# Moving the first denominator group of each half by four slots, and taking the last quad's first reciprocal from the bank

## The reference

```python
q = Wq @ layernorm(x) + bq;  k = Wk @ ctx + bk;  v = Wv @ ctx + bv
dot = mask * (q . k) / sqrt(32) - (1 - mask) * 1e6
amap = softmax(dot, axis=-1) * mask          # a row maximum, exp, and a denominator
x = x + tanh(g_xattn) * (amap @ v)
x = x + tanh(g_ffn) * fp8_product(layernorm(x), W2)
```

## Time and profile before

| | us |
|---|---|
| median of 3 runs | 2485.4 (2483.09 to 2494.34) |
| the profiled execution, its own time | 2483.92 |
| its span, first to last instruction | 2482.1 |
| TensorE busy | 2406.5 |
| VectorE busy | 1934.1 |
| ScalarE busy | 1401.9 |
| GpSimd busy | 1714.9 |
| mean granted TensorE clock | 0.994 of full |

### The profile page before, as it was taken

The page is one execution under the profiler, slowest core; times in us unless marked ns, Lnnn a source line. Parts: engine busy times, 40 slices in busy tenths (PEclk is TensorE's granted clock), DMA queues, the critical chain, the costliest instruction groups (busy, mean ns, idle before and its releaser), DMA issues. The chain is left out here.

```text
span 2482.1 us, 40026 instructions
## 1 busy us (share of the span) xinstructions
PE 2406.5 (97%) x12612; PEld 1362.3 (55%) x12673; DVE 1934.1 (78%) x3196; ACT 1401.9 (56%) x2702; POOL 1714.9 (69%) x1413
## 2 busy tenths in 40 slices
PE   7999999999999999999999999999999999999996
PEld 5888888875444444444444444444444444444442
DVE  6777666677788888888888888888888888888874
ACT  3333333325666666666666666666666666666663
POOL 2443333436887878888887888888788787878873
PEclk9999999999999999999999999999999999999998
DMA  6766666665566666666666666666666666666633
GB/s 238 256 241 234 232 235 233 237 204 145 121 128 141 134 133 129 139 139 137 128 130 131 138 135 128 127 131 137 137 129 129 137 139 129 133 135 138 139 75 73
DMA packets 265487, 380.57 MB, mean 153 GB/s; under 512 B 77688, under 2 KB 145336, under 8 KB 257112
## 3 DMA queue, kind: packets, MB, share of 16 engines
q1 hardware_dynamic: 245240, 275.57, 46.1%
q0 software_dynamic: 9216, 67.11, 13.5%
q10 hardware_dynamic: 10848, 35.66, 4.1%
HBM read 199.83 MB, written 101.38 MB: 121 GB/s over the span
## 5 line engine op out<-in xcount | busy, mean ns | idle before, releaser
L1251 DVE TENSOR_REDUCE part_max<-bank 128x1 f32<-128x512 f32 x2048 | 1282.8, 683 | 254.0 <-PE bank L978 247.5
L790 ACT ACTIVATE probs<-bank 128x512 f32<-128x512 f32 x2048 | 1077.6, 602 | 595.9 <-PE bank L961 579.4
L961 PE MATMUL bank<-q_st,k_st 100*128 100x512 f32 x2048 | 866.9, 425 | 4.5 <-ACT probs L790 3.3
L978 PE MATMUL bank<-k_st,q_st 98*128 98x512 f32 x2048 | 816.6, 399 | 6.0 <-DVE part_max L1251 4.7
L441 POOL TENSOR_TENSOR pair_sum<-probs 128x512 f32<-128x512 f32 x512 | 641.9, 1283 | 134.3 <-ACT probs L790 134.1
L961 PEld LDWEIGHTS bank<-q_st,k_st 100*128 100x128 f32 x2048 | 387.2, 189 | 411.7 <-issue 190.3
L993 PE MATMUL bank<-probs,v_t 128*32 128x512 f32 x4096 | 545.5, 605 | 0.0
L978 PEld LDWEIGHTS bank<-k_st,q_st 98*128 98x128 f32 x2048 | 387.9, 189 | 128.2 <-DVE part_max L1251 19.1
L441 POOL TENSOR_TENSOR stage_hi<-probs 128x512 f32<-128x512 f32 x252 | 316.1, 1287 | 75.6 <-ACT probs L790 75.4
L441 POOL TENSOR_TENSOR stage<-probs 128x512 f32<-128x512 f32 x252 | 318.2, 1325 | 24.9 <-ACT probs L790 24.9
L402 POOL TENSOR_TENSOR stage_lo<-stage,stage_hi 128x512 fp32r<-128x512 f32 x128 | 188.3, 1492 | 137.8 <-ACT stage_hi L735 136.7
(11 more groups left out here) (121 smaller groups left out, 2360.1 us busy)
## 6 DMA issues: line engine op xcount, KB each, us to landing
pair_sum<-pair_sum POOLq DMA_DIRECT2D x64, 1024.0 KB, 8.5
k_st<-k_scr SPq DMA_DIRECT2D x192, 256.0 KB
q_st<-q_scr SPq DMA_DIRECT2D x192, 256.0 KB
c_raw<-in_ctx_dram ACTq DMA_DIRECT2D x32, 512.0 KB, 7.0
k_scr<-stage_hi SPq DMA_DIRECT2D x64, 256.0 KB, 2.5
k_scr<-stage_lo SPq DMA_DIRECT2D x64, 256.0 KB, 2.7
v_scr<-stage SPq DMA_DIRECT2D x64, 256.0 KB, 2.9
q_scr<-stage_hi SPq DMA_DIRECT2D x64, 256.0 KB, 2.4
```

The source lines that it names most:

```text
L790: nc.scalar.activation(probs[:, c % PR, h, :], s_bank_of(n, k)[:, :], ACT.Exp).then_inc(exp_done, 1)
L961: nc.tensor.matmul(s_bank_of(n, k)[:, :], k_st[p][0:KS, h, j * P:(j + 1) * P], q_st[p][0:KS, th, h, :], start=True, stop=True).then_inc(sc ...
L978: nc.tensor.matmul(x_bank_of(n, "tile", k)[:, :], q_st[p][0:KX, th, h, tc * P:(tc + 1) * P], k_st[p][0:KX, h, sh * HALF:(sh + 1) * HALF], ...
L1251: nc.vector.tensor_reduce(part_max[:, th, at:at + 1, sh], x_bank_of(n, "tile", k)[:, :], AX, ALU.max).then_inc(max_done, 2)
```

## The change

The first group of each half is issued at slots 31 and 63 in place of 27 and 59. In the last quad alone, the copy, the two moves through HBM, the small reciprocal and the mask product of the first half are left out; VectorE takes the reciprocal of all 512 columns from d_bank and multiplies by mask and gate, in its queue at slot 45. The pair 6 products of the last quad (`denominators_last(SJ - 2)`, with the first group of the half, so at slot 63 too) wait for that reciprocal in place of the copy.

```diff
-            DEN_AT = {27: 0, 35: 1, 43: 2, 59: 3}
+            DEN_AT = {31: 0, 35: 1, 43: 2, 63: 3}
...
-                            if r == (5 if n == LAST else 6) and real(n):
+                            if r == 6 and ordinary(n):
                                 mask_inverse(n, 0)
...
-                        if real(n):
+                        if ordinary(n):
                             move_den(n, 0)
...
-                        if real(n):
+                        if ordinary(n):
                             move_inv(n, 0)
                             spread_inv(n, 0)
...
-                            if k == 44 and real(n):
+                            if k == 44 and ordinary(n):
                                 copy_den(n, 0)
...
                         if r == SJ - 2:
-                            pe.wait_ge(den_copied, 2 * LAST + 1)
+                            pe.wait_ge(last_inverse, 1)
...
+                    def invert_last():
+
+                        dve.wait_ge(den_done, NG * LAST + GROUPS_0)
+                        dve.wait_ge(half_weighed, LAST)
+                        nc.vector.reciprocal(inv_b[:, 0], d_bank[:, :]).then_inc(last_inverse, 1)
+                        dve.wait_ge(last_inverse, 1)
+                        nc.vector.scalar_tensor_tensor(inv_b[:, 0], inv_b[:, 0], g1[:, 0:1], m_b[:, 0:HALF], ALU.mult,
+                                                       ALU.mult).then_inc(last_inverse, 1)
...
-                        dve.wait_ge(inv_spread[0], 16 * (m + 1))
+                        dve.wait_ge(last_inverse, 2)
...
-                        if k == 51 and real(n):
+                        if k == 51 and ordinary(n):
                             invert(n, 0)
+                        if k == 45 and n == LAST:
+                            invert_last()
```

More of the change, by code:

```diff
@@ L202, in flamingo_gated_layer @@
         half_weighed = sem("half_weighed")
+        last_inverse = sem("last_inverse")
         norm_done = sem("norm_done")
@@ L325, in flamingo_gated_layer @@
             F_JOBS = {23: "max1", 39: "ffn0", 51: "ffn1", 55: "max0"}
-            DEN_AT = {27: 0, 35: 1, 43: 2, 59: 3}
+            DEN_AT = {31: 0, 35: 1, 43: 2, 63: 3}
             DEN_AFTER = {3: 4, 11: 5}
-            NG = 6
+            NG, GROUPS_0 = 6, 3
             SUM_OF_GROUP = (2, 1, 3, 6, 5, 7)
```

## The result

The change makes the kernel 0.29% slower by the recorded ratio, 1.0029 with a 95% interval of 1.0021 to 1.0036. The medians are 2492.04 us over 20 runs and 2486.48 over 20 runs of the kernel before beside them (5.6 us, or 0.22%, apart). Of the latter, one run took 3821.61 us and the others 2480.2 to 2494.3; the ratios here go by the fast runs alone. The prediction was 2485 and no change. The profiled execution has a span of 2492.4 us at a mean clock of 0.992, 10.3 above the one before.

What follows compares the result with a forecast made beforehand. TensorE, busy 97%, was taken to bound the kernel: its queue plus its waits. 2483.92 + 4 (steady part) - 3.5 (finish) = 2484.4, given as 2485 with the median's offset; range 2468 to 2497 for 8 times in 10.

Steps and rivals of the forecast that it cites:

- no change: Whole kernel: 2485 us; a measurement was said to tell 0.5%, 12 us, from no change; chance of same 0.7.
- the bank wait: Slots 63 and 31: fourth score tile waits for VectorE's late maximum; per period 0.25 us lost at 63, 0.07 gained at 31.
- rival 2: Slots 59 to 63: GpSimd's adds shut out VectorE's L93, about 5 us each; chance 0.03 all periods (2634), 0.07 some.
- rival 1: Slots 63 and 31: the bank wait doesn't bite, 2456 us, chance 0.13; a half of it, about 2470, chance 0.11.
- rival 3: Slots 31 and 63: denominators come too late for their later uses, some 0.5 us per period, 2500 us; chance 0.02.
- some odd period: Single periods: GpSimd's adds shut VectorE out, +5 us in a single one, 2490 to 2510; chance 0.07.
- the margin of 0.48: Behind slot 59: L93 starts at 1444.66, 0.48 us ahead of GpSimd's pair 7 adds at 1445.14, so it gets in first.
- One add at most: Port pair shared by VectorE and GpSimd: by the skill's lock rule, VectorE would lose one GpSimd add at most.
- The term of -3.5: Last quad's finish: residual lands 3.2, say 3.5 us earlier, without the spread inverse's wait; bounds 0.8 to 8.0.
- the 0.9 that I had taken off: Finish: 0.9 us off the residual load's 6.5, as it no longer shares queues with the spread's 256 KB.
- The steady sum: Slots 63 and 31 over all periods: about +4 us; bounds -24.5 to +10.7.
- the 1.25 for quads 0 and 1: Three groups (quad 0 both halves, quad 1 the first) without VectorE steps beside them: win 0.46 + 0.33 + 0.46 us.

Runs made afterwards that it cites:

- Experiment 5: The changed kernel with quad 1's group at slot 59 and VectorE's four steps (L90, L93, L100, L101) cut to 128 of 1024 columns above quad 0: 2461.45 us, ratio 0.9907.
- the control of experiment 5: The kernel before, groups at slots 27 and 59, with the same four VectorE steps cut to 128 of 1024 columns: 2483.58 us, ratio 0.9998.
- experiment 3: The changed kernel with, in quad 1 alone, the second half's first group back at slot 59: 2487.36 us, ratio 1.0004 to the kernel before.
- experiment 1: Each half alone against the kernel before: moved slots only, 2499.03 us, ratio 1.0048; last quad's inverse only, groups at 27 and 59, 2479.33 us, ratio 0.9970.
- experiment 6: VectorE's steps spread, last quad changed; L95 cut at 512 or 768 columns. Moved groups (quad 1's at 59): 0.9971, 0.9937; old slots: 1.0027, 0.9995, against the kernel before.

## Why the prediction was wrong

**What held.** The group starts without a wait; slots 63 and 31 have the bank wait; the stretches moved by +0.25 (forecast +0.25) and by -0.10 (forecast -0.07); L1324 (L1314 before) waits for nothing, L1327 (L1317 before) for the residual. Experiment 5 and its control show that this wait is the cause. It was not the whole-period version of rival 2, nor rival 1, nor rival 3.

**What failed first: rival 2 in "some odd period".** I gave it a chance of 0.07 and 5 us, and nothing in the sum. It comes in quad 1 in every kernel profiled whose group stands at slot 63 there (7.26, 7.53, 7.31 and 7.28 for L90) and in none with it at 59. It costs 8.0 us in the trace and about 6 by the runs (experiment 3). Both the price and the place were off. Beside the standstill of 6.9 us, products and group then ran at half clock. And two parts of my reasoning let it through. I weighed the margin of 0.48 in one period and took it for all, though GpSimd is later against TensorE in quad 1: in the kernel before, its sum for `stage` is ready 2.52 behind the start of the products of slot 59 there, and 1.06 in a usual period. And I looked at L93 against the adds of pair 7, while it was L90, begun amid those of pair 6, that counted. The wait that I took away was what gave GpSimd its pause. Why GpSimd is late just in quad 1 stays open. It has no feed-forward products yet (the first one comes at 718.8 us in the kernel before), but quad 0 has none either, and there the sum is 1.20 behind; no run adds or removes them.

The Trainium skill (SBUF — State Buffer, "SBUF: two separate sides") has the port pair that VectorE and GpSimd share as a lock: whoever starts first holds it for the instruction, and the other is blocked in full. The trace agrees with the block: L90 took 7.26 us against 0.68. "One add at most" was my own step from it, and that failed: L90 was shut out over the end of one block of adds and the whole of another, though each add is an instruction of its own, and it ended only behind GpSimd's last one.

**What failed second: the finish.** The term of -3.5 (3.2 by its parts, rounded up) measured -5.9 in the trace and about -7.5 by the runs (bounds 0.8 to 8.0). The store was 1.5 earlier, the number forecast, but by luck: I put it down to the moved group, and 1.2 of it comes with the group at its old slot too (experiment 1, and the control of experiment 5), because what it makes up is the fall of the clock in the one execution I read. I took that fall, the 1.93 in place of 1.07, for a cost of the old slot. Mis-sized was the store's landing, kept at 8.9: issued ahead of the merge instead of behind it, it took 4.5, and 3.3 to 4.8 in the twelve other kernels, which all issue it ahead. With the detour in place this brings the finish from 69.9 to 67.8 or 68.0 only; with the reciprocal from the bank it is 62.6 to 64.0 in every kernel. So the change itself is worth about 4 of the 5.9, and the order of store and merge and the clock the other 2. The residual's load stayed at 6.5 and gave nothing of the 0.9 that I had taken off. The added reciprocal cost VectorE's chain 3.36 + 0.96, and GpSimd waited 0.69 for it. Its merge went out 28.1 us behind slot 23 rather than 27.6, but the last denominators ended no later for it (39.6, and 39.7 in the control of experiment 5).

**The steady sum.** I had +4. By experiments 1 and 3, the moved slots without quad 1's loss cost 1.0004 - 0.9970 = 0.34%, some 8 us, with an uncertainty of about 3. By typical values, 30 x 0.25 - 29 x 0.10 - 1.25 is about 3.5. The loss at slot 63 came out in full: the 29 stretches 55 to 23 behind quad 1 sum to 7.3 us more. The gain at slot 31 didn't: all stretches 23 to 55 sum to 964.8 us against 964.2. Those hold the feed-forward products, and their sum scatters (967.0 with the last quad's change alone, whose slots are those of before), so single profiles can't tell whether it was there. Of the 1.25 for quads 0 and 1 the trace shows 0.50, at slot 63 of quad 0.

**The size that I took for "no change".** I wrote that a measurement tells 12 us from none. With 20 runs on either side the interval is 0.08% to either side, 2 us, so a sum of small terms with a lean to one side was within reach of it.

**Together:** forecast +4 - 3.5 = +0.5. By the trace: quad 1 +8.0, the other stretches +7.3 (of which the typical values explain about 3.5), the finish -5.9, and 0.9 ahead of the first of these stretches: +10.3. By the runs: +0.29%.

## What to carry to other kernels

A wait that is removed may have been the pause in which another engine got at a shared resource; look at each period that differs from the usual, the first and last above all, and not at the margin in one. Moving work away from a long step of a helper engine exposes that step: move or cut the step in the same change, each piece clearly shorter than what then covers it (0.86 us under 1.0 of products still cost 0.1). For transfers on the last path, look at what is issued just ahead: here it doubled the landing time. And before a long instruction in one profile becomes a term, look at the granted clock beside it.

## What the runs showed of the hardware that was not expected

- A TENSOR_SCALAR of 128x1024 on VectorE (0.68 us alone) took 7.26 us beside GpSimd's fp32 adds that followed one another without a pause, and 1.92 to 2.65 where it began 1.3 to 2.1 us ahead of the end of such a block and a pause came behind it. In both cases it ended some 0.57 behind the block.
- A TENSOR_TENSOR of 128x512 in fp32 on VectorE is held up far less: 1.16 us for 0.69, while GpSimd's four adds took 5.46 for some 5.0. Whether the two shared or took turns isn't shown. One of 128x1024 in bf16 (L101, 0.69 alone) was shut out as well: 5.67 to 5.73 us in the last quad of the four kernels of experiment 6.
- While TensorE stood still for 6.9 us its granted clock fell to half (0.50 of full) and stayed there until about 693 us, and a block of products took 1.94 for 1.06.
- The same 512 KB store landed in 8.9 us behind a merge of 1 MB, and in 3.3 to 4.8 ahead of it in thirteen other kernels.
